# Two products of the second layer in float32r parts, one copy moved to ScalarE, and a reordered schedule, in a hand-scheduled transformer block

## The reference

```python
Xn = layernorm(X) * ln_g + ln_b
Q, K, V = split_heads(Xn @ Wq + bq), split_heads(Xn @ Wk + bk), split_heads(Xn @ Wv + bv)
A = softmax(where(causal, Q @ K.T / sqrt(16), -inf))
x1 = layernorm(X + (A @ V) @ Wo + bo)

h = relu(x1 @ W1 + b1)                       # the first dense layer, 256 -> 256
alpha = softmax(h @ W2 + b2)                 # 8 weights per row
vx = einsum('krd,bsd->bskr', V, x1)          # the middle space, 256 -> 8 x 64 = 512
out = layernorm(x1 + einsum('bsk,bskd->bsd', alpha, einsum('kdr,bskr->bskd', U, vx)))
```

## Time and profile before

| | |
|---|---|
| median of 3 runs | 442.87 us (442.53 to 443.21) |
| the profiled execution | 442.42 us, span 440.7 us |
| granted TensorE clock, mean | 0.998 |
| busy: PE, DVE, ACT, POOL | 94%, 70%, 53%, 17% of the span |

### The profile page before, as it was taken

The page is one execution under the profiler, slowest core; times in us unless marked ns, Lnnn a source line. Parts: engine busy times, 40 slices in busy tenths (PEclk is TensorE's granted clock), DMA queues, the critical chain, the costliest instruction groups (busy, mean ns, idle before and its releaser), DMA issues.

```text
span 440.7 us, 7218 instructions
## 1 busy us (share of the span) xinstructions
PE 413.6 (94%) x2515; PEld 204.3 (46%) x2515; DVE 307.7 (70%) x821; ACT 235.1 (53%) x509; POOL 73.9 (17%) x111
## 2 busy tenths in 40 slices
PE   7998899999999989999999999999999998998994
PEld 3545344343334433366547844334334443336663
DVE  4638996798798783437378799789879873114465
ACT  5681554666668576443441265666676847542321
POOL 3430210233120110102230021113312010010000
PEclk9999999999999999999999999999999999999999
DMA  6076761350402000001764037045040000000011
GB/s 191 12 105 95 179 100 20 58 88 3 74 2 97 2 1 0 1 0 52 129 116 65 1 80 103 13 62 86 10 67 3 0 3 1 1 1 0 1 48 48
DMA packets 18435, 21.13 MB, mean 48 GB/s; under 512 B 4960, under 2 KB 11872, under 8 KB 18400
## 3 DMA queue, kind: packets, MB, share of 16 engines
q1 hardware_dynamic: 18349, 20.66, 25.0%
q10 hardware_dynamic: 51, 0.01, 0.0%
HBM read 5.79 MB, written 2.10 MB: 18 GB/s over the span
## 4 chain that ended last, share of the span: by engine, by line
PE 67%; DVE 20%; ACT 7%; issue 2%; DMA 1%; POOL 1%; DVEq 0%; ACTq 0%; POOLq 0%
PE ps L842 27%; PE ps L947 13%; DVE mx L725 13%; PE ps L927 11%; PE ps L904 8%; DVE ps L721 3%; ACT pr L606 2%; PE ps L833 2%; PE ps L849 2%; PE ps L992 1%; PE ps L908 1%; PE ps L957 1%; DMA stq<-mrow 1%; ACT stk L549 1%; ACT qk_raw L592 1%
## 5 line engine op out<-in xcount | busy, mean ns | idle before, releaser
L606 ACT ACTIVATE pr<-ps 128x512 f32<-128x512 f32 (+3 forms) x384 | 165.6, 497 | 105.7 <-PE ps L927 104.3
L725 DVE TENSOR_REDUCE mx<-ps 128x1 f32<-128x512 f32 (+3 forms) x240 | 145.6, 664 | 13.1 <-PE ps L904 6.6
L927 PE MATMUL ps<-stq,stk 99*128 99x512 bf16 (+3 forms) x384 | 116.4, 330 | 5.8 <-ACT pr L606 4.4
L904 PE MATMUL ps<-stk,stq 96*128 96x512 bf16 (+3 forms) x384 | 112.9, 327 | 2.5 <-DVE mx L725 1.3
L540 POOL TENSOR_SCALAR_AFFINE_SELECT pr<-pr 128x512 f32<-128x512 f32 x64 | 40.6, 635 | 255.3 <-ACT pr L606 255.3
L947 PE MATMUL ps<-pr,va 128*32 128x512 f32 (+3 forms) x768 | 81.8, 498 | 0.0
L927 PEld LDWEIGHTS ps<-stq,stk 99*128 99x128 bf16 x384 | 34.6, 97 | 94.4 <-ACT pr L606 56.8
L904 PEld LDWEIGHTS ps<-stk,stq 96*128 96x128 bf16 x384 | 37.5, 98 | 23.2 <-issue 6.5
L721 DVE CUSTOM_DVE_ANT_0 ps<-ps,causal 128x384 f32<-128x384 f32 (+1 forms) x64 | 38.5, 647 | 13.2 <-PE ps L904 13.2
L908 PE MATMUL ps<-mask,ident_b 128*128 128x128 bf16 x192 | 35.4, 219 | 0.0
L842 PE MATMUL ps<-u_t,avt 128*128 128x256 f32 x128 | 30.8, 383 | 0.2 <-ACT avt L628 0.2
(11 more groups left out here) (90 smaller groups left out, 380.1 us busy)
## 6 DMA issues: line engine op xcount, KB each, us to landing
stq<-qk_raw SPq DMA_DIRECT2D x32, 96.0 KB, 2.8
stk<-qk_raw SPq DMA_DIRECT2D x32, 96.0 KB, 2.8
x_in<-in_x SPq DMA_DIRECT2D x8, 256.0 KB, 3.5
stq<-qk_raw SPq DMA_DIRECT2D x32, 64.0 KB, 2.4
stk<-qk_raw SPq DMA_DIRECT2D x32, 64.0 KB, 2.4
out_y<-x SPq DMA_DIRECT2D x3, 512.0 KB, 3.0
stk<-qk_raw SPq DMA_DIRECT2D x32, 32.0 KB, 2.4
stq<-qk_raw SPq DMA_DIRECT2D x32, 32.0 KB, 2.1
```

Of the source, the lines that this page charges most:

```text
L606: nc.scalar.activation(probs(b, g, s)[:, j, q0 - c * CHUNK:], act_bank(ev)[:, q0 - c * CHUNK:], ACT.Exp, scale=DH ** -0.5).then_inc(s_act_ ...
L725: nc.vector.tensor_reduce(dst, src, AX.X, ALU.max).then_inc(s_dve_free, 1)
L904: last = nc.tensor.matmul(bank[:, i * w:(i + 1) * w], q[0:ROWS, t // TPC, j, tile(t % TPC)], k[0:ROWS, k0 // CHUNK, j, 0:w], start=True, s ...
L927: nc.tensor.matmul(bank[:, q0 - c * CHUNK:], stk[stack_of(b, g)][0:ROWS + PARTS, kt // TPC, j, tile(kt % TPC)], stq[stack_of(b, g)][0:ROWS ...
```

## The change

- `w_1` and `v_t` are kept twice, as `float32r`: a near part (ScalarE rounds the whole weight on copying it, event `halve`) and a far part (VectorE subtracts the near part from the whole, event `far`). The whole weights land in `avt` and `avx`. Four `halve` and four `far` events stand beside steps 24 to 29 of batch 0, each `far` two steps behind its `halve`.
- `x1t`: ScalarE's copy writes the near part of x1 (signalled on `s_near`), VectorE subtracts it from the bank and writes the far part. The bank now comes from VectorE's ring.
- `h` and `vx`: in place of two float32 products over k there are six float32r ones: near x near, far weight x near (for `vx` near x far), and the remaining cross product; far x far is left out. In `h` the four that need only the near x1 come first, the two that need the far one last.
- `rows`: ScalarE copies the bank into `mrow` in place of VectorE, and the bank comes from ScalarE's ring.
- `va` has 17 columns a head in place of 32 and is set to one as a whole (128x2432 elements; before 128x2048); the value product still loads 32 columns, of which the last 15 belong to the next head.
- Order beside the attention: `x1t`, `h`, `lg`, `alpha`, `vx` and `avt` of chunk 0 stand one step earlier, `r1` and `ln2` slightly later, the next batch's `ln1` of chunk 0 after `h` (step 41) in place of step 38. Both `ln2` are in `quick`.
- Tail: `u` 0 stands behind the last `turn`, `avt` 2 behind `ot`, `u` 3 between `x1t` and `h`, and `ln3` goes by single tiles for two tiles.

```diff
-        beside = {35: res[0][:parts], 36: res[0][parts:parts + 1], 37: res[0][parts + 1:], 41: mix[0][0], 42: mix[0][1][:parts], 43: mix[0][1][parts:], 44: [("alpha", b, 0)] + m[0][:1], 45: m[0][1:2],
-                  46: m[0][2:4], 47: m[0][4:5] + m[0][6:7], 48: m[0][5:6], 49: m[0][7:8]}
+        beside = {35: res[0][:parts], 36: res[0][parts:parts + 1], 37: res[0][parts + 1:-1], 38: res[0][-1:], 40: mix[0][0],
+                  41: mix[0][1][:parts], 42: mix[0][1][parts:], 43: [("alpha", b, 0)] + m[0][:1], 44: m[0][1:2],
+                  45: m[0][2:4], 46: m[0][4:5] + m[0][6:7], 47: m[0][5:6], 48: m[0][7:8]}
+        if nb == batches:
+            beside[47] = beside[48] = []
         if nb < batches:
-            beside[38] = [("ln1", nb, 0, TPC)]
+            beside[41] = beside[41] + [("ln1", nb, 0, TPC)]
...
+            for i, (name, k) in enumerate((name, k) for name in ("1", "vt") for k in ks):
+                beside[24 + i] = beside.get(24 + i, []) + [("halve", 0, name, k)]
+                beside[26 + i] = beside.get(26 + i, []) + [("far", 0, name, k)]
...
-            order += ot + [r4, r6, n] + m[0][8:11] + turned + mixed[:-2] + m[0][11:] + mixed[-2:]
-            order += [("alpha", b, 1)] + m[1][:2] + third[b][:1] + m[1][2:-3] + [("ln3", b, TPC, 2)] + m[1][-3:] + [("ln3", b, TPC + 2, 2)]
+            order += m[0][5:6] + ot + m[0][7:8] + [r4, r6, n] + m[0][8:11] + turned + m[0][11:] + mixed
+            order += [("alpha", b, 1)] + m[1][:2] + third[b][:1] + m[1][2:7] + [("ln3", b, TPC, 1)] + m[1][7:9] + [("ln3", b, TPC + 1, 1)]
+            order += m[1][9:] + [("ln3", b, TPC + 2, 2)]
...
-    quick = [ev for ev in order if ev == ("ln1", 0, 0, TPC) or ev[0] == "ln2" and ev[2] >= TPC
+    quick = [ev for ev in order if ev == ("ln1", 0, 0, TPC) or ev[0] == "ln2"
...
-            pool.memset(va[:, :, :, DH:], 1.0).then_inc(s_ones, 1)
+            pool.memset(va_rows[:], 1.0).then_inc(s_ones, 1)
...
+                if kind == "halve":
+                    _, _, name, k = ev
+                    whole, split = split_weights[name]
+                    act.wait_ge(s_w[name], 16)
+                    nc.scalar.activation(split[:, 0, k], whole[:, k], ACT.Copy).then_inc(s_weight_near, 1)
+                if kind == "x1t":
+                    _, _, c, k = ev
+                    act.wait_ge(s_dve_full, n_dve[ev])
+                    nc.scalar.activation(x1_t[:, 0, k, :], dve_bank(ev), ACT.Copy).then_inc(s_near, 1)
...
+                    nc.scalar.activation(mrow[:, c, :], act_bank(ev)[0:PARTS * HPG * TPC, 0:P], ACT.Copy).then_inc(s_act_free, 1)
...
+                if kind == "far":
+                    _, _, name, k = ev
+                    whole, split = split_weights[name]
+                    dve.wait_ge(s_weight_near, n_halve["halve", *ev[1:]])
+                    nc.vector.tensor_tensor(split[:, 1, k], whole[:, k], split[:, 0, k].bitcast(F32),
+                                            ALU.subtract).then_inc(s_weight_far, 1)
+                if kind == "x1t":
+                    _, _, c, k = ev
+                    dve.wait_ge(s_near, n_near[ev])
+                    nc.vector.tensor_tensor(x1_t[:, 1, k, :], dve_bank(ev), x1_t[:, 0, k, :].bitcast(F32),
+                                            ALU.subtract).then_inc(s_dve_free, 1)
...
-                nc.vector.tensor_copy(mrow[:, c, :], dve_bank(ev)[0:PARTS * HPG * TPC, 0:P]).then_inc(s_dve_free, 1)
...
-                    product(bank, lambda k: w_1[:, k, tile(m)], lambda k: x1_t[:, k, :], KC,
-                            lambda k: ("x1t", b, c, k)).then_inc(s_act_full, 1)
+                    sides = lambda i, k: w_1[:, i, k, tile(m)], lambda j, k: x1_t[:, j, k, :]
+                    pe.wait_ge(s_near, n_near["x1t", b, c, KC - 1])
+                    part_products(bank, *sides, ((0, 0), (1, 0)), KC, start=True)
+                    pe.wait_ge(s_dve_free, n_dve["x1t", b, c, KC - 1])
+                    part_products(bank, *sides, ((0, 1),), KC, stop=True).then_inc(s_act_full, 1)
...
-                    product(bank, lambda k: x1_t[:, k, tile(t % TPC)], lambda k: v_t[:, k, :], KC).then_inc(s_dve_full, 1)
+                    part_products(bank, lambda i, k: x1_t[:, i, k, tile(t % TPC)], lambda j, k: v_t[:, j, k, :],
+                                  ((0, 0), (0, 1), (1, 0)), KC, start=True, stop=True).then_inc(s_dve_full, 1)
```

More of the change, by code:

```diff
@@ L10 @@
 BF16 = mybir.dt.bfloat16
+F32R = mybir.dt.float32r
 I32 = mybir.dt.int32
@@ L307, in block_kernel @@
         o_sb = y = x1
+        whole_1 = avt[:].rearrange("p i (k d) -> p (i k) d", d=D)[:, 0:KC]
+        whole_vt = avx[:]
+        split_weights = {"1": (whole_1, w_1), "vt": (whole_vt, v_t)}
         early_x, early_xh = ([qk_raw[:, w, c, 0:TPC * D].rearrange("p (t d) -> p t d", d=D) for c in range(C)] for w in range(2))
@@ L337, in block_kernel @@
         s_dve_free = sem("s_dve_free")
+        s_weight_near = sem("s_weight_near")
+        s_weight_far = sem("s_weight_far")
+        s_near = sem("s_near")
         s_high = sem("s_high")
@@ L355, in count @@
             return {ev: n + 1 for n, ev in enumerate(e for e in order if e[0] in kinds)}
-        n_act = count("xt", "v", "score", "ot", "x1t", "h", "avt")
-        n_dve = count("qk", "fold", "max", "rows", "turn", "r1", "lg", "vx", "u")
+        n_act = count("xt", "v", "score", "rows", "ot", "h", "avt")
+        n_dve = count("qk", "fold", "max", "turn", "r1", "lg", "x1t", "vx", "u")
+        n_near, n_halve, n_far = count("x1t"), count("halve"), count("far")
         n_high, n_part = count("qk"), count("part")
@@ L479, in _ @@
                         weight(w_o[:], wo, "o")
-                        weight(w_1[:], w1, "1")
+                        weight(whole_1, w1, "1")
                         weight(w_2[:], w2, "2")
-                        weight(v_t[:], vt, "vt")
+                        weight(whole_vt, vt, "vt")
                         weight(u_t[:], ut, "ut")
@@ L735, in _ @@
                     if b * G + g:
-                        dve.wait_ge(s_dve_full, n_dve["rows", *divmod(b * G + g - 1, G), c])
+                        dve.wait_ge(s_act_full, n_act["rows", *divmod(b * G + g - 1, G), c])
                     link(nc.vector.tensor_copy(mhl[:, c, 0], whole))
@@ L843, in product, with part_products @@
                 return last
+            def part_products(out_, lhs, rhs, which, n, start=False, stop=False):
+                terms = [(i, j, k) for i, j in which for k in range(n)]
+                for i, j, k in terms:
+                    last = nc.tensor.matmul(out_, lhs(i, k), rhs(j, k), start=start and (i, j, k) == terms[0],
+                                            stop=stop and (i, j, k) == terms[-1])
+                return last
             def turn_over(bank, n):
@@ L858, in _ @@
                     _, _, c, k = ev
-                    bank = take_act(ev)
+                    bank = take_dve(ev) if kind == "x1t" else take_act(ev)
                     by_tile = ()
@@ L870, in _ @@
                         src = x1[:, c * TPC:(c + 1) * TPC]
-                    turn(bank, src, k, *(by_tile if k == 0 else ())).then_inc(s_act_full, 1)
+                    turn(bank, src, k, *(by_tile if k == 0 else ())).then_inc(s_dve_full if kind == "x1t" else s_act_full, 1)
                     if ev == ("xt", 0, 0, KC - 1):
@@ L984, in _ @@
                     bank = take_dve(ev)
[L985 to L986 removed]
+                    if b == 0:
+                        pe.wait_ge(s_weight_far, n_far["far", 0, "vt", KC - 1])
+                    part_products(bank, lambda i, k: x1_t[:, i, k, tile(t % TPC)], lambda j, k: v_t[:, j, k, :],
+                                  ((0, 0), (0, 1), (1, 0)), KC, start=True, stop=True).then_inc(s_dve_full, 1)
                 if kind == "avt":
```

41 lines of the change are left out of this document (21 added, 20 removed).

## The result

| | before | after |
|---|---|---|
| median of the runs | 442.88 us (442.53 to 443.21) | 436.66 us (436.31 to 437.0) |
| profiled execution, its own time | 442.42 us | 436.52 us |
| its span | 440.7 us | 434.8 us |

The ratio is 0.986, 95% interval 0.9843 to 0.9877: faster by 6.2 us, where 11.0 us were forecast. The prediction's direction and range (428 to 439 us) hold; its number, 431.9 us, is 4.8 us too low, and the time lies outside the likeliest case's own range (428 to 435 us).

The account below looks back on a forecast made before the run. TensorE's queue sets the pace in the layer's second half, VectorE from 120 to 137 us; 10.1 + 2.0 - 0.4 - 0.7 + 0.5 + 1.7 - 1.9 - 0.3 = 11.0 us gained, giving 431.9 us, range 428 to 439 us.

Parts of the forecast that it names:

- likeliest case: The forecast itself, 431.9 us, with its own range of 428 to 435 us and a chance of 0.73.
- The products: `h` and `vx`: float32r takes one stream, 0.216 us a product; 24 events fall from 1.72 to 1.30 us, gaining 10.1 us.
- rivals 2 and 3: `h` and `vx`: float32r at half speed, 463 us, chance 0.09; or run as float32, 525 us, 0.03 with its like.
- The weight loads are not the limit: `h` and `vx`: a load of 128 float32 columns takes 190 ns, and `u` holds 0.218 us a record with such loads.
- The subtractions: Four weight subtractions on VectorE, where it has 0.46 us of slack in 17, cost 2.2 us: -1.9 us.
- The rows: VectorE loses 16 copies of 0.275 us, three of eight a batch counted where maxima set the pace: +1.7 us.
- The new place of `h`: Steps 40 and 41: an earlier `h` shortens the wait for ScalarE, 1.0 us a batch, +2.0 us.
- the end of the attention: Batch 1: `u` 0 fills the 0.97 us the transposes waited for VectorE, the last value waits: +0.5 us net.
- The tail: `u` 3 covers the copy of x1, but `lg` waits about 0.95 us and `avt` 4 some 0.3: -0.7 us.
- rival 1: VectorE's far copies, subtractions and the near-then-far handoff stand on the path: 437.4 us, 434.5 to 441 us; chance 0.15.
- The bank of the second `h` in chunk 1 of batch 0: The second `h` starts when ScalarE's copy frees its bank, so a faster first `h` only waits: -0.4 us.
- The beginning: VectorE's first statistics wait for GpSimd's fill of `va`, which grows from 1.80 to 2.14 us: -0.3 us.

Follow-up runs that it names:

- Experiment 3: The changed kernel with far by far added to each `vx`, eight float32r products in place of six: 445.4 us.
- experiments 2: The changed kernel with seven unread bfloat16 products put into TensorE's wait for the split (group 2, chunk 1, batch 0): 437.48 us.
- experiment 4: The changed kernel with the fill of `va` moved behind GpSimd's fill and select of the causal mask: ratio 0.985.
- experiment 6: The changed kernel with the old order beside the attention and in the tail; float32r parts and `rows` on ScalarE stay: 437.59 us.
- experiment 1: The changed kernel with the four weight subtractions moved from steps 26 to 29 to steps 37 and 39: 435.14 us, ratio 0.982.
- experiment 5: The changed kernel with the copies of the rows of maxima given back to VectorE and its ring: 440.74 us.
- experiment 7: The changed kernel with the second `r1` and `ln2` of chunk 0 back in step 37 in both batches: 437.63 us.
- experiment 8: The changed kernel with later weight subtractions, later `va` fill, `ln2` in step 37, and the tail's near products of both `h` first: 435.13 us.

## Why the prediction was right, and where its number was off

- **The products: the right mechanism, a term mis-sized.** "I take one stream: the float32 product shows four streams" held, and rivals 2 and 3 fell: 1.40 us an event, not 2.61 or 5.18. But the event was put at 1.30 us from the bfloat16 row. The 24 events gave 24 x 0.32 = 7.7 us by this pace, not 10.1; this is 2.4 of the missing 5.1 us, 0.6 in each of four lines of the table. Experiment 3 shows that pace apart from everything else. "The weight loads are not the limit" is open: twelve loads of `vx` in 2.65 us are 0.221 us each, close to the pace, `u` held 0.218 us a record with such loads, and no run separated the two.
- **The Trainium skill**, page "FP8 and Floating Point Precision", section "TensorE Precision Notes", gives true float32 four passes and has reduced precision truncate its four bytes; taken as one pass this gives the same 1.30 us, an estimate, for the page has no pace for it. The run shows 0.1 us an event more, and so agrees with one pass and not with four.
- **The subtractions: right by themselves, but a wait's second price was missed.** 1.8 us against the 1.9 forecast (experiments 2, 4, 6). The forecast took the delay of the split as a delay alone. It also left TensorE busy 0.51 of 2.60 us, and the half clock behind that cost 1.5 us. The sizes of the single instructions were sound: 682 ns for the large form (forecast 690), and 0.42 and 0.73 us for the two of the small one (forecast 0.42), which took 0.42 and 0.43 us in their later place in experiment 1.
- **The rows: too small by 0.7 us.** "By their place in the list I count three of eight a batch": the six copies up to step 27 of batch 0 alone were worth 1.5 us. The stretches that hold them gained 1.6 and 0.8 us, 2.4 in all against 1.7; experiment 5 gives 2.3 without its longer half clock.
- **The new place of `h`: 0.6 us in batch 0, 0.2 in batch 1 with the end of the attention, against 1.0 and 1.5.** In batch 0 the steps of the reckoning nearly held: with the 2.29 us taken off by which the kernel was already late, `h` begins at 161.2 us (forecast 160.8) and TensorE is through with `turn` at 166.5 us (forecast 166.0). The wait for the near copy (0.48 us), which the prediction named as a danger, is small. `ln2` was later than reckoned, but experiment 7 shows that this alone cost nothing. The step that failed is that batch 1 would do as batch 0: there the second `h` kept its wait for a relu, and `lg` came 0.6 us later. At the end of the attention I had priced one new wait and found two (0.50 and 0.72 us), more than the 0.97 us that went.
- **The tail.** The wait of `lg` was forecast as 0.95 us and measured as 0.87. Not forecast: far copies in VectorE's queue behind residuals and statistics, about 0.3 us inside `h` in the changed kernel (3.46 us for its twelve products, 3.14 in experiment 8). Together 1.2 us of waits where before had 0.34, so of 1.9 us of products 1.0 to 1.1 should be left, and 1.0 was measured. This is rival 1 in small: 1.2 us of net waits with the order of before (experiment 6), 0.9 us with the new one, and not 5.5 us. The total lies in that rival's range, but not by its mechanism: more than a quarter of what is missing is a clock that no term named. That 436.66 us stands inside 428 to 439 us is luck in part, for the room above 435 us had been left for rival 1.
- **The bank of the second `h` in chunk 1 of batch 0** is as forecast: it waits 0.63 us for ScalarE's copy where it waited 0.30, so the first `h`'s 0.32 us went there, and the stretch gained 1.4 us for 1.9 of products.
- **The beginning:** the statistics began 0.33 us later, as forecast. The first value product was 0.61 us late; that the fill as a whole had a price, 1.5 us (experiment 4), and that the warm-up decides how much of it can be had, was not seen.

By measured terms: 7.7 (products) - 1.2 (the parts' handoffs in the tail, with the order of before) + 1.4 (new order) - 0.5 (bank) + 2.4 (rows) - 3.3 (subtractions with the clock) - 0.6 (beginning) = 5.9 us, the measured difference of the spans; each term is good to some 0.2 us.

## What to carry to other kernels

- Price a new wait of TensorE twice: by its length, and by what the clock may cost behind it. Here a wait of about 2 us (1.96 in the changed kernel) with nothing put into it was followed by 3.4 us or more at half clock in three profiled executions and by none in three others; 3.4 us of it cost 1.4 to 1.7 us of time. Products that nothing reads, put into the wait ahead of its semaphore, stood in the three kernels whose filled waits kept the full clock; that they are the reason is likely and not shown. A stretch of half clock can turn up elsewhere in the next version and hide what that version gained, so compare marks ahead of it.
- Take a new data type's pace from a kernel of its own or keep its bounds wide: 8% on a product, with 144 of them on the path, was half of the error.
- A queue in front of an engine that is "half idle" still delays: VectorE's far copies and ScalarE's near copies were free by load and late by order. Compare marks by stretch, not totals, to see this, and first take off by how much the kernel is late where the stretch begins.
